# Gated delta attention on one core: GpSimd's key work moved behind the score products, VectorE's order cut anew, sigmoid ahead of widening

## The reference

```python
q = l2norm(x @ Wq) / sqrt(K); k = l2norm(x @ Wk); v = x @ Wv; gate = x @ Wg
beta = sigmoid(x @ Wb); g = cumsum(-exp(A_log) * softplus(x @ Wa + dt_bias))
L = where(tril, exp(g_i - g_j), 0)
P = where(strict, (k * beta) @ k.T * L, 0)
Ainv = I + P + P^2 + ...            # applied to v*beta and to k*beta*exp(g)
# then, chunk after chunk, with the state S:
v_new = v - kcd @ S
o = (q * exp(g)) @ S + (q @ k.T * L) @ v_new
S = S * exp(g_last) + (k * exp(g_last - g)).T @ v_new
# out = (rmsnorm(o) * norm_w * silu(gate)) @ Wo
```

## Time and profile before

| | |
|---|---|
| median of 3 runs | 1225.05 us (1222.36 to 1228.53) |
| profiled execution | 1227.84 us, span 1225.6 us |
| busy: TensorE / VectorE / ScalarE / GpSimd | 83% / 77% / 49% / 33% of the span |
| granted TensorE clock, mean | 0.93 of full speed |
| attention stage (slots 0 to 39) | about 223 to 829 us of the span |

### The profile page before, as it was taken

One profiled execution on the slowest core, in us unless ns is written; L12 is line 12 of the kernel. 1 busy time (PEld: TensorE's weight loads), 2 busy tenths in 40 slices (PEclk: granted clock), 3 DMA queues, 4 the chain that ended last, 5 costly groups with the idle time before them and its releaser, 6 DMA issues. The chain is left out here.

```text
span 1225.6 us, 38519 instructions
## 1 busy us (share of the span) xinstructions
PE 1020.6 (83%) x15510; PEld 738.3 (60%) x15510; DVE 941.6 (77%) x2432; ACT 599.6 (49%) x1614; POOL 407.9 (33%) x580
## 2 busy tenths in 40 slices
PE   2999977876888887889878886679999886799968
PEld 2888863444555555556555665457888774255546
DVE  3777736368999999999888897726887546899976
ACT  2433336443677676777667665554433253200134
POOL 3666630311222212222222121224665448400037
PEclk9999988888999999999998987779999988899979
DMA  9000013244444444444444443200000023946003
GB/s 254 19 2 1 1 39 130 64 91 99 102 105 98 92 88 100 107 104 89 87 98 106 97 88 76 47 11 1 2 1 1 1 61 90 267 115 172 1 18 121
DMA packets 282625, 93.31 MB, mean 76 GB/s; under 512 B 208976, under 2 KB 275408, under 8 KB 282448
## 3 DMA queue, kind: packets, MB, share of 16 engines
q1 hardware_dynamic: 247056, 84.03, 28.6%
q10 hardware_dynamic: 35392, 6.82, 2.9%
HBM read 56.20 MB, written 30.41 MB: 71 GB/s over the span
## 5 line engine op out<-in xcount | busy, mean ns | idle before, releaser
L1772 DVE TENSOR_TENSOR delta_tmp<-delta_PR 128x130 f32<-128x130 f32 (+12 forms) x416 | 153.0, 368 | 9.4
L1769 DVE TENSOR_TENSOR delta_PR<-delta_PR,delta_tmp 128x130 f32<-128x130 f32 (+12 forms) x416 | 152.2, 366 | 9.3
L1422 PE MATMUL psum<-delta_T,delta_pad 128*32 128x128 f32 x2048 | 84.2, 333 | 33.0 <-DMA delta_T<-inverse_scratch 31.8
L1884 POOL TENSOR_TENSOR delta_S<-delta_E,delta_Bm 128x128 f32<-128x128 f32 x32 | 15.3, 477 | 285.2 <-issue 276.4
L1621 ACT ACTIVATE delta_y<-psum 32x128 f32<-32x128 f32 x256 | 68.7, 268 | 84.7 <-PE psum L1456 56.8
L1422 PEld LDWEIGHTS psum<-delta_T,delta_pad 128*32 128x32 f32 x2048 | 71.8, 134 | 42.8 <-DMA delta_T<-inverse_scratch 39.2
L506 POOL TENSOR_TENSOR ffn_H<-ffn_hid,ffn_H 128x512 fp32r<-128x512 f32 x48 | 61.8, 1292 | 57.6 <-DVE ffn_H L472 57.6
L1406 PE MATMUL psum<-delta_MV,delta_KT 32*32 32x128 f32 x2048 | 70.4, 291 | 11.7 <-ACT delta_E L1571 11.7
L1637 ACT ACTIVATE delta_wide<-delta_S 32x128 f32<-32x128 f32 x256 | 78.2, 305 | 3.2
L506 POOL TENSOR_TENSOR first_H<-first_hid,first_H 128x512 fp32r<-128x512 f32 x48 | 61.7, 1292 | 53.4 <-DVE first_H L472 53.4
L1406 PEld LDWEIGHTS psum<-delta_MV,delta_KT 32*32 32x32 f32 x2048 | 60.2, 114 | 22.8 <-ACT delta_E L1571 15.9
(11 more groups left out here) (278 smaller groups left out, 2586.6 us busy)
## 6 DMA issues: line engine op xcount, KB each, us to landing
within_scratch<-delta_PT SPq DMA_DIRECT2D x128, 64.0 KB, 1.9
delta_PR<-within_scratch SPq DMA_DIRECT2D x16, 512.0 KB, 4.6
inverse_scratch<-delta_PR SPq DMA_DIRECT2D x16, 512.0 KB, 3.0
space_T<-taps_scratch SPq DMA_DIRECT2D x8, 1024.0 KB, 5.9
X<-taps_scratch SPq DMA_DIRECT2D x8, 1024.0 KB, 8.8
X<-in_x SPq DMA_DIRECT2D x32, 128.0 KB, 10.0
turned_scratch<-gates_XT SPq DMA_DIRECT2D x16, 256.0 KB, 2.3
delta_xT<-turned_scratch SPq DMA_DIRECT2D x32, 128.0 KB, 3.8
```

The lines of the kernel that those rows point to most:

```text
L1422: i = pe.matmul(bank[3][SUB * c:SUB * c + SUB, (2 * w + g) * P:(2 * w + g + 1) * P], M.pad[:, from_c:from_c + SUB], M.T[t % 2][:, h * P:(h ...
L1769: i = v.tensor_tensor(after, after, t3, ALU.add)
L1772: i = v.tensor_tensor(t3, column.to_broadcast([P, j, n_after]), row.to_broadcast([P, j, n_after]), ALU.mult)
```

## The change

Five edits, all in the attention stage.

- GpSimd: the key work of tile n, and `fade_first` for the next scan tile ahead of it, wait for the score products of the slot (`f_kk`); `fade_first` moves from the start of the next slot to this place. `middle_state` waits for X (`s_x`) where it waited for Bm (`s_bm`).
- SyncE: `keys_out` and `keys_in` handle a tile one slot later than before.
- ScalarE: `sigmoid_g` runs ahead of `widen(Z, 1)`.
- VectorE: `add_o` and `new_stats` of an output tile move from the end of its slot to the start of the next one; X follows Bm with no step between; the substitution is cut at other places (8 steps instead of 10 ahead of `scale_qk`, 13 instead of 15 ahead of `keep_gate`, 25 instead of 24 ahead of `keep_within`).
- The last `add_o` stands behind the loop.

```diff
--- before.py
+++ after.py
@@ -1341,8 +1341,8 @@
     for n in range(SLOTS):
         at(rows_in, n + 1)
         at(decays_in, n)
-        at(keys_out, n - 1)
-        at(keys_in, n - 2)
+        at(keys_out, n - 2)
+        at(keys_in, n - 3)
         at(within_out, n - LAG_FORM)
         if n % 2 == 0:
             if 0 <= (n - 2) // 2 < NT // 2:
@@ -1663,9 +1663,9 @@
             inverse_in(a, B, M, S, n - LAG_APPLY, (2, 3), S.i_late)
         at(keep_y, Z, 1)
         at(root_qk, n)
-        at(widen, Z, 1)
         at(keep_v, n)
         at(sigmoid_g, n)
+        at(widen, Z, 1)
         at(exp_decays, n - LAG_FORM)
         at(keep_ot, n - LAG_OUT)
         at(keep_wt, n - LAG_APPLY)
@@ -1813,31 +1813,30 @@
     for n in range(SLOTS):
         Z, O = n - LAG_SCAN, n - LAG_OUT
         at(own_heads, Z, 0)
-        solve(n, 0, 1)
         at(new_state, Z, 0)
-        solve(n, 1, 3)
+        at(add_o, O - 1)
         at(sum_qk, n)
-        solve(n, 3, 6)
+        if O - 1 < AHEAD * BLK:
+            at(new_stats, O - 1)
+        solve(n, 0, 4)
         at(faded_q, n - LAG_FORM)
-        solve(n, 6, 10)
+        solve(n, 4, 8)
         at(scale_qk, n)
-        solve(n, 10, 11)
+        solve(n, 8, 9)
         at(own_heads, Z, 1)
-        solve(n, 11, 12)
+        solve(n, 9, 10)
         at(new_state, Z, 1)
-        solve(n, 12, 15)
+        solve(n, 10, 13)
         at(keep_gate, n)
-        solve(n, 15, 21)
+        solve(n, 13, 22)
         at(sum_o, Z)
-        solve(n, 21, 24)
+        solve(n, 22, 25)
         at(keep_within, n - LAG_FORM)
-        solve(n, 24, 25)
+        solve(n, 25, 26)
         at(keep_attn, n - LAG_FORM)
-        solve(n, 25, 29)
+        solve(n, 26, 29)
         at(scale_o, Z)
-        at(add_o, O)
-        if O < AHEAD * BLK:
-            at(new_stats, O)
+    add_o(NT - 1)
 
 
 def delta_gpsimd(g, own, B, M, S, run):
@@ -1878,7 +1877,7 @@
 
     def middle_state(t):
         g.wait_ge(S.s_e, 2 * t + 1)
-        g.wait_ge(S.s_bm, 2 * t + 1)
+        g.wait_ge(S.s_x, 2 * t + 1)
         if t > 0:
             g.wait_ge(S.s_wide, 2 * t)
         g.tensor_tensor(M.S1, M.E0, M.Bm, ALU.add).then_inc(S.s_1, 1)
@@ -1894,10 +1893,12 @@
 
     for n in range(SLOTS):
         Z = n - LAG_SCAN
-        at(fade_first, Z)
         at(middle_state, Z)
         at(fade_second, Z)
         at(gate_o, n - LAG_OUT)
+        if 0 < n <= NT:
+            g.wait_ge(S.f_kk, n)
+        at(fade_first, Z + 1)
         at(decayed_k, n)
         at(kept_k, n)
         if n in (SLOTS - 4, SLOTS - 3):
```

## The result

The changed kernel takes 1236.55 us (median of 8 runs, 1232.23 to 1241.64); the kernel before, on the same chip, takes 1223.14 us (8 runs, 1219.66 to 1228.53). The ratio is 1.0109 with a 95% interval of 1.008 to 1.0139: slower by 13.4 us. The forecast was 1226, no change, with a range that ended at 1236. The profiled execution took 1236.07 us, 8.2 us more than that of before; slots 8 to 31 alone grew by more than that.

The account below looks back on a forecast made before the run. VectorE's work and a once-a-pair trip through five engines and queues were taken to bind together. Terms -0.45 - 0.03 + 0.67 gave +0.2 us a pair, +2.4 in 12 pairs, less 1.5: +0.9, forecast 1226 us, range 1211 to 1236.

Parts of the forecast that it names:

- the odd slot's term of the sum: Odd slot, start to its PT: VectorE's work in order, 12.81 us before, 12.83 us after the change.
- the 3.19 us from the even PT to the slot: VectorE behind the even PT: 3.95 us less 0.33 (add_o) and 0.43 (one step), 3.19 us.
- Even slot, L1704 to PT: VectorE's paid work in even slots: L1704 to gate 3.21 to 2.46 us, gate to PT 4.17 to 5.87 us.
- The trip from odd PT to L1704: Stores, inverse's loads and root between odd PT and even L1704: 8.94 us in the sum, 9 to 10 us as sign.
- Stretch behind L1704: VectorE steps beside GpSimd's key work: -1.3 us a pair, back ahead of PT +0.5 (even), +0.35 (odd); net -0.45.
- X: VectorE's difference at the slot's start, beside GpSimd's sum: falls from 0.54 to 0.28 us.
- The other wait of `middle_state`: GpSimd waits for X instead of Bm: net -0.03 us a pair, X's lost stretch included.
- the sigmoid's place: ScalarE's sigmoid ahead of widen: 0, since VectorE's position sets the gate; outputs covered with 0.2 us to spare.
- The keys' edit on SyncE: Keys_out and keys_in one tile later, same five DMAs at the same place of each slot: 0.
- Waits: TensorE's wait for the gate falls, for the inverse's DMA not; VectorE's idle before L1721 in odd slots goes.
- the "slower" rival: Odd slots: late inverse load, cold TensorE, apply ending later than 8.4 us into the slot; +11 us, 1236 us; chance 0.25.
- The "faster" rival: GpSimd's stretch of VectorE comes out whole: 0.65 + 0.35 us a slot less 0.5, -12 us, 1213; chance 0.34.

Follow-up runs that it names:

- rest_bm: `rest_only` with GpSimd's `middle_state` waiting for Bm as before instead of X: 1214.25 us, ratio 0.9896.
- rest_widen_first: `rest_only` with ScalarE's old order, `widen` ahead of `keep_v` and `sigmoid_g`: 1209.18 us, ratio 0.9895.
- rest_only: The changed kernel with VectorE's old order, all other edits kept: 1211.95 us, ratio 0.9906 against the kernel before.
- rest_no_hold: `rest_only` without GpSimd's wait for the score products, key work right behind `scale_qk`, `fade_first` behind it: 1221.9 us, ratio 0.9985.
- warm: The changed kernel with 12 idle 128x128 products on TensorE ahead of `apply` of odd tiles 3 to 25: 1232.46 us, ratio 1.0093.
- pt_early: The changed kernel with PT after 22 substitution steps instead of 25 in every slot, `sum_o` after 20 instead of 22: 1220.24 us, ratio 0.9966.
- vec_only: The kernel before with VectorE's new order alone; GpSimd, SyncE and ScalarE as before: 1244.47 us, ratio 1.017.

## Why the prediction was wrong

**The step that failed** is the odd slot's term of the sum, 12.83 us from its start to its PT, taken as VectorE's own work less a small wait. With the 3.19 us from the even PT to the slot it says 16.02 us from PT to PT, 0.74 less than the 16.76 of the pair that I had followed. Measured, on the mean of 12 pairs, it went from 17.11 (10.45 + 3.24 + 3.42) to 17.30 us (10.59 + 2.98 + 3.73): +0.19. The odd slot's term itself, from its start to its PT, measured 14.13 us (12.82 before). The difference, 0.93 us a pair and 11.2 us over 12, is more than the whole error of these slots (10.9 us measured against 2.4 forecast); the even work and the trip behind the odd PT came out slightly better than in the sum. In the even slot I shortened the stretch behind PT from 3.95 to 3.19 us and booked it as a gain, but the load of the inverse starts from PT too. In the mean it needs 10.5 us to `apply` however VectorE's work is cut, so what is removed behind the even PT comes back as a wait in the odd slot. I had followed the trip of the odd PT through the queues and had not followed the same trip of the even PT. The small wait of L1721 in the earlier trace rows (3.1 us) did not mean that VectorE alone set the odd slot: the load and VectorE's own work arrived close together, and a later load showed at once.

**The other steps.**
- Even slot, L1704 to PT: forecast +0.95 us (-0.75, +1.70), measured 7.39 to 8.27, +0.88. Right, and in both of its parts: to the gate forecast 2.46 us, measured 2.40; from there to PT forecast 5.87, measured 5.87.
- The trip from odd PT to L1704: forecast 9 to 10 us, measured 9.48. Right. VectorE's wait there was forecast above 18 us, and measured 14.0 (8.3 before); the late odd PT is not what shortens it, since it is counted from that PT. The direction was right, and the size was not.
- Stretch behind L1704 gone and partly back ahead of PT: right. In slot 20 it comes to 0.24 + 3 x 0.08 = 0.48 us, forecast 0.5. By the Trainium skill (SBUF — State Buffer, § SBUF: two separate sides) a VectorE step with two SBUF inputs that starts behind a GpSimd instruction that reads SBUF is blocked fully until that one ends. Here the four steps ran beside GpSimd's keys and `fade_first`, over 2 us of work, and the largest of them lost 0.24 us: the trace decides against it here.
- X: forecast 0.28 us, measured 0.29. The other wait of `middle_state` and the sigmoid's place were forecast at 0; `rest_bm` and `rest_widen_first` don't differ from `rest_only`. Right within what 5 runs tell. The keys' edit on SyncE was forecast at 0 too; with the hold there is no wait for it, without the hold there is (`rest_no_hold`).
- Waits: that for the gate fell as said. That for the inverse was said not to fall; it nearly doubled. The idle time in front of L1721 was said to go, and stayed at 3.1 us; the over 5 us that were to mark the "slower" rival did not come either.
- The rival "slower" had the place right (the odd slot's load, 9 of 12 `apply` runs slow, keys at full price in even slots) and its price, 1236, was near the result. Its point of decision was that `apply` ends later than 8.4 us into the odd slot. Since `apply` starts 10.59 us behind a PT that stands 3.17 us ahead of the slot, its start alone is at 7.4 us and its end at 10.5; the start could be had from the trace of before with the forecast's own 3.19 us (10.45 - 3.19 = 7.3 us). There the end was on average at 10.45 - 4.29 + 2.63 = 8.8 us already, past the point of decision. With this sum the rival would have been the forecast.
- What the rival had in addition, the lower clock, gave back 4 us by the medians (`warm`), under a third of the loss.

The "faster" rival's price came out for the half without VectorE's new order: `rest_only` took 1211.95 us, near its 1213. That is in part luck: the rival counted on the stretch alone, and of the 1.2 us a pair by which `rest_only` is shorter only 0.63 lie between L1704 and the even PT.

**A version that beats both** is the changed kernel with VectorE's old order (`rest_only`, 1211.95 us; `widen` first, 1209.18, is no different within the noise): 1% below the kernel before. It was found by undoing the part that was meant to accompany the hold.

**Open.** Why taking out the hold costs some 3 us, not clear of the noise, in the new order and 10 us in the old one was not isolated. `pt_early` and `rest_only` have the same even work but differ by 8 us in slots 8 to 31, of which the trip to L1704 is 0.6 us a pair; what makes that trip longer was not tried. Untried as well is the edit that the theory suggests: in even slots, SyncE's `inverse_in` ahead of `within_out`. The odd tile's part lay in DRAM from the start of slot 20 on (ScalarE's load at 529.92 waited for that landing), and in the kernel before SyncE loaded its half at 545.13, behind the stores of PT.

## What to carry to other kernels

Where a pipeline of several slots hands work through DRAM, mark every trip through queues, where it starts and what else stands ahead of it in the queue, for each parity of the slot; between two trips only the work ahead of the next start is paid, and a step moved behind it is free until another loop takes over. Two arrivals that take turns as the last show as small waits on both sides: a small wait there is no slack. A change with several parts is best timed in halves, since here one half gained 11 us and the other lost 21. A run that takes one edit out must be looked at for what the edits left in do without it: `rest_no_hold` got a wait that neither kernel had.

## What the hardware did that I had not expected

**The landing of the same stores varied by 2 us.** In slot 20 of the changed kernel SyncE issues PT's four stores and then waits for their landing before the next load:

```profile
545.23 1.93 SPq L1339 DMA_DIRECT2D within_scratch<-delta_PT  x4
550.61 0.34 SPq L1328 DMA_DIRECT2D delta_PR<-within_scratch  x1
551.05 0.92 SPq L1282 DMA_DIRECT2D delta_T<-inverse_scratch  x2
```

The load of the pair comes 6.15 us behind PT (544.46). In the same slot of the kernel before it came 4.16 us behind:

```profile
541.30 1.93 SPq L1339 DMA_DIRECT2D within_scratch<-delta_PT  x4
544.69 0.34 SPq L1328 DMA_DIRECT2D delta_PR<-within_scratch  x1
545.13 1.65 SPq L1282 DMA_DIRECT2D delta_T<-inverse_scratch  x2
```

One slot misleads here. Over all 12 even slots this stretch is 4.15 to 5.97 us before (mean 4.95) and 4.15 to 6.15 us after (mean 5.20). ScalarE issues its half of the odd tile's load while the stores are under way, in the changed kernel (546.73 in slot 20):

```profile
546.73 0.32 ACTq L1282 DMA_DIRECT2D delta_T<-inverse_scratch  x1
547.08 0.54 ACTq L1282 DMA_DIRECT2D delta_T<-inverse_scratch  x1
```

That these loads delay the landing is not borne out: in slot 18 of `vec_only` they come 2.78 us behind PT and the pair's load after 4.15 us, in slot 22 of `rest_only` 3.90 us behind PT and the pair's load after 6.18 us. What sets the landing stays open.

**Stretch goes both ways.** GpSimd's own key work is longer too after the change, in slot 20 (0.62 and 0.90 us in the earlier trace rows, where it met VectorE's steps as well):

```profile
542.48 0.77 POOL L1859 TENSOR_TENSOR delta_VK<-delta_QK,both_eg 128x256 f32<-128x256 f32 x1
543.21 1.07 POOL L1869 TENSOR_TENSOR delta_Kd_tok<-delta_QK,both_bekd 128x128 f32<-128x128 f32 x2
```

**TensorE's clock after a wait.** `apply` follows 4.51 us of waiting in slot 21 and takes 3.44 us, where with the idle products of `warm` ahead it takes 1.95 us; the granted clock of the slot was 0.91 of full speed, and the two levels are 1.2 and 2.4 GHz. The length of the wait alone does not decide: in slot 19 of the changed kernel `apply` follows 2.75 us of waiting and takes 3.64 us, in slot 15 it follows 3.24 us and takes 1.96 us.
